# Bias of layer h of a graph layer: two matmuls on TensorE, or a table of columns added by ScalarE

## The reference

```python
h = relu(layernorm(x))
S = h[src]                                     # one row per edge
def edge_nn(x, W, b):
    h = relu(x @ W.T + b)                      # "layer h"
    return relu(h @ W.T + b)                   # "layer m"
msgs = edge_nn(S, W_rel[rel], b_rel[rel])      # rel of each edge is 0 or 1
agg = segment_sum(msgs, dst)
i, f, g, o = split(agg @ W_ih.T + b_ih + b_hh)
hn = sigmoid(o) * tanh(sigmoid(i) * tanh(g))
return x + mlp(hn)                             # 256 -> 128 -> 128 -> 256
```

## Time and profile before

| | |
|---|---|
| median of 3 runs | 2260.63 us (2260.33 to 2261.53) |
| the profiled execution | 2269.79 us, its span 2268.1 us |
| PE busy | 2080.7 us, 92% |
| DVE busy | 1755.9 us, 77% |
| ACT busy | 1627.2 us, 72% |
| POOL busy | 1187.8 us, 52% |
| mean granted TensorE clock | 0.959 of full |
| moved by DMA | 396.90 MB, mean 175 GB/s |

### The profile page before, as it was taken

How to read it: one execution, slowest core, us unless ns; L and a number is a source line. 1 busy time by engine, 2 the same in 40 slices (tenths; PEclk the granted TensorE clock), 3 DMA queues, 4 the chain that set the end, 5 groups by cost and what they waited for, 6 DMA issues and landing times.

```text
span 2268.1 us, 51837 instructions
## 1 busy us (share of the span) xinstructions
PE 2080.7 (92%) x14224; PEld 1405.7 (62%) x14225; DVE 1755.9 (77%) x4311; ACT 1627.2 (72%) x3364; POOL 1187.8 (52%) x917
## 2 busy tenths in 40 slices
PE   5858767767999999999999999999999999999996
PEld 4746555555666666666666666666666666445553
DVE  8537555555888888888888888888888887788886
ACT  2437655555888888888888888888888887666663
POOL 0036777777766665666666666666666644100000
PEclk7559999898999999999999999999999999999998
DMA  9954555557789898889888988888888988988886
GB/s 383 425 207 93 95 95 100 98 97 141 135 174 185 170 180 174 179 170 175 175 178 173 178 177 180 178 178 183 170 178 175 180 153 162 193 188 191 190 188 156
DMA packets 400606, 396.90 MB, mean 175 GB/s; under 512 B 263738, under 2 KB 343158, under 8 KB 394360
## 3 DMA queue, kind: packets, MB, share of 16 engines
q0 software_dynamic: 91200, 157.34, 40.8%
q1 hardware_dynamic: 306788, 238.12, 40.0%
q10 hardware_dynamic: 2516, 0.14, 0.1%
HBM read 185.88 MB, written 156.97 MB: 151 GB/s over the span
## 4 chain that ended last, share of the span: by engine, by line
PE 78%; issue 7%; POOL 5%; ACT 3%; DMA 3%; DVE 3%; another core or an unknown queue 1%; POOLq 0%; DVEq 0%; ACTq 0%; SPq 0%
PE bank L1469 33%; PE bank L1435 9%; PE bank L1416 9%; PE bank L1483 6%; PE bank L1508 5%; PE bank L1452 4%; PE bank L1398 3%; PE bank L1492 3%; POOL agg L664 2%; POOL xg L648 2%; DMA agg<-summed,scatter_idx 2%; PE bank L1308 2%; PE bank L1409 2%; PE bank L1427 1%; DMA a_lo<-row_lo 1%
## 5 line engine op out<-in xcount | busy, mean ns | idle before, releaser
L664 POOL DMA_INDIRECT agg<-summed,scatter_idx x400 | 665.5, 1664 | 501.4 <-ACT summed L724 261.4
L1469 PE MATMUL bank<-a_hi,ihT 128*128 128x512 f16 x2400 | 714.0, 379 | 2.4 <-DMA a_lo<-row_lo 2.2
L648 POOL DMA_INDIRECT xg<-in_x,src_ring x400 | 426.1, 1065 | 271.0 <-DMA src_ring<-src_slot 138.1
L1469 PE MATMUL bank<-a_lo,ihT 128*128 128x512 f16 x1200 | 454.8, 379 | 0.0
L1469 PEld LDWEIGHTS bank<-a_hi,ihT 128*128 128x128 f16 x2400 | 234.4, 98 | 213.0 <-issue 2.3
L1435 PE MATMUL bank<-relT,h_hi 128*128 x1600 | 321.5, 275 | 0.0
L1416 PE MATMUL bank<-s_hi,relT 128*128 128x256 f16 x1600 | 292.9, 278 | 0.0
L672 POOL DMA_DIRECT2D y<-in_x x100 | 133.4, 1334 | 298.0 <-DVE y L1202 287.6
L1077 DVE SCALAR_TENSOR_TENSOR h_lo<-bank,h_hi 128x512 f16<-128x512 f32 x200 | 137.5, 688 | 120.4 <-ACT h_hi L751 114.6
L757 ACT ACTIVATE xn<-xg,shift,rstd 128x256 f32<-128x256 f32 x400 | 216.4, 591 | 10.3 <-DVE shift L1111 10.3
L1070 DVE SCALAR_TENSOR_TENSOR s_lo<-bank,s_hi 128x512 f16<-128x512 f32 x200 | 136.4, 682 | 111.2 <-ACT s_hi L730 73.4
(11 more groups left out here) (197 smaller groups left out, 4642.4 us busy)
## 6 DMA issues: line engine op xcount, KB each, us to landing
agg_in<-agg SPq DMA_DIRECT2D x100, 512.0 KB
y<-in_x POOLq DMA_DIRECT2D x100, 512.0 KB
out<-y SPq DMA_DIRECT2D x100, 512.0 KB
agg<-zeros SPq DMA_DIRECT2D x24, 2112.0 KB, 15.8
dst_ring<-dst_rows SPq DMA_DIRECT2D x200, 128.0 KB
xg<-in_x,src_ring POOLq DMA_INDIRECT x400
agg<-summed,scatter_idx POOLq DMA_INDIRECT x400
src_ring<-src_slot SPq DMA_DIRECT2D x200, 1.0 KB
```

Of the source, the lines that this page charges most:

```text
L648: nc.gpsimd.indirect_dma_start(out=xg[:, k.slot(8), t, :], out_offset=None, in_=x[:, :], in_offset=bass.IndirectOffsetOnAxis(ap=src_ring[: ...
L664: nc.gpsimd.indirect_dma_start(out=agg[:, :], out_offset=bass.IndirectOffsetOnAxis(ap=scatter_idx[:, k.slot(8), t:t + 1], axis=0), in_=sum ...
L1469: last = nc.tensor.matmul(N_C[c % 2][:, 0:UNIT], lhs, rhs, start=i == 0, stop=i == len(todo) - 1)
```

## The change

In joint steps PE no longer adds layer h's bias. A table `pair_bias` of 400 columns is made once, two columns per pair, each with 128 features of the bias of that pair's relation. ACT applies Relu with such a column as bias, one instruction for each of the two column halves, into a new f32 tile `h_f` in SBUF (one buffer). DVE casts `h_f` to `h_hi` and subtracts to get `h_lo`. PE's wait for the bank is then on `h_f_ready`, ACT's write of `h_f` waits until DVE has made `h_lo` of the pair before, and DVE's cast waits for `m_done` of two pairs before. On DVE the cast comes ahead of `hidden`, and `low_h` moves behind it. Edge-only steps, and layer m's bias, stay as they are. In the diff the first `high_h` is ACT's, `low_h`, the second `high_h` and the table are DVE's, and `layer_h` is PE's.

```diff
-WEIGHT_LOADS = 14
+WEIGHT_LOADS = 15
...
+            act.dma_start(brel_col[:, :, :], b_rel.rearrange("r (c p) -> p r c", p=P)).then_inc(weights_in, 16)
...
             def high_h(k):
                     act.wait_ge(h_done, k.n + 1)
-                    nc.scalar.activation(h_hi[:, k.slot(2), :], B_H[k.bank][:, :], ACT.Relu).then_inc(h_hi_ready, 1)
+                    if k.both:
+                        if k.is_(NB):
+                            act.wait_ge(pair_bias_ready, 1)
+                        act.wait_ge(h_ready, k.n)
+                        for m in range(KH):
+                            half = slice(m * PAIR, (m + 1) * PAIR)
+                            last = nc.scalar.activation(h_f[:, half], B_H[k.bank][:, half], ACT.Relu,
+                                                        bias=pair_bias[:, bass.ds(k.n * KH + m, 1)])
+                        last.then_inc(h_f_ready, 1)
+                    else:
+                        nc.scalar.activation(h_hi[:, k.slot(2), :], B_H[k.bank][:, :], ACT.Relu).then_inc(h_hi_ready, 1)
...
+            chained(alternate)
+            nc.vector.tensor_scalar(other_rel[:, :], pair_rel[:, :], 0.0, None, ALU.is_equal).then_inc(pair_rel_ready, 1)
+            dve.wait_ge(pair_rel_ready, 1)
+            dve.wait_ge(weights_in, 16 * WEIGHT_LOADS)
+            for m in range(KH):
+                last = nc.vector.tensor_scalar(other_bias[:, :, m], other_rel[:, :], brel_col[:, 0, m:m + 1], None, ALU.mult)
+            chained(last)
+            for m in range(KH):
+                last = nc.vector.scalar_tensor_tensor(out=bias_of[:, :, m], in0=pair_rel[:, :], scalar=brel_col[:, 1, m:m + 1],
+                                                      in1=other_bias[:, :, m], op0=ALU.mult, op1=ALU.add)
+            last.then_inc(pair_bias_ready, 1)
...
             def low_h(k):
+                    if k.both:
+                        dve.wait_ge(h_hi_ready, k.n + 1)
+                        nc.vector.tensor_tensor(h_lo[:, k.slot(2), :], h_f[:, :], h_hi[:, k.slot(2), :],
+                                                ALU.subtract).then_inc(h_ready, 1)
...
+            def high_h(k):
+                if k.within(PAIRS):
+                    dve.wait_ge(h_f_ready, k.n - NB + 1)
+                    wait_from(dve, m_done, k.n - 1)
+                    nc.vector.tensor_copy(h_hi[:, k.slot(2), :], h_f[:, :]).then_inc(h_hi_ready, 1)
...
+                if (at - 1).both:
+                    high_h(at - 1)
+                hidden(k, half)
                 low_h(at - 1)
-                hidden(k, half)
...
             def layer_h(k, r):
-                wait_from(pe, h_ready, k.n if k.both else k.n - 1)
+                if k.is_(NB):
+                    pe.wait_ge(h_ready, k.n)
+                elif k.both:
+                    pe.wait_ge(h_f_ready, k.n - NB)
+                else:
+                    wait_from(pe, h_ready, k.n - 1)
...
-                    nc.tensor.matmul(ps, brel_parts[:, bass.ds(r * D + m * P, P)], ones16[:, :], start=True, stop=False)
+                    if not k.both:
+                        nc.tensor.matmul(ps, brel_parts[:, bass.ds(r * D + m * P, P)], ones16[:, :], start=True, stop=False)
...
-                        last = nc.tensor.matmul(ps, lhs, rhs, start=False, stop=i == len(todo) - 1)
+                        last = nc.tensor.matmul(ps, lhs, rhs, start=k.both and i == 0, stop=i == len(todo) - 1)
```

More of the change, by code:

```diff
@@ L218, in build @@
         spare_row = sb("spare_row", [P, 2])
-        pair_start = sb("pair_start", [1, PAIRS])
+        pair_start = sb("pair_start", [P, PAIRS])
         iota_tile = sb("iota_tile", [P, TILES])
@@ L228, in build @@
         dst_slot = sb("dst_slot", [P, TILES])
-        pair_rel = sb("pair_rel", [1, PAIRS], I32)
+        pair_rel = sb("pair_rel", [P, PAIRS], I32)
+        pair_bias = sb("pair_bias", [P, PAIRS * KH])
         unit_row = sb("unit_row", [1, UNITS], I32)
@@ L243, in build @@
         gate_b = sb("gate_b", [P, 8])
+        brel_col = sb("brel_col", [P, NUM_REL, KH])
         b1_col = sb("b1_col", [P, 1])
@@ L295, in build @@
         quarter_row = tmp("quarter_row", [1, QUARTERS])
-        flips = tmp("flips", [1, 2, PAIRS])
+        flips = tmp("flips", [P, 2, PAIRS])
+        other_rel = tmp("other_rel", [P, PAIRS])
+        other_bias = tmp("other_bias", [P, PAIRS, KH])
         slot = tmp("slot", [ROWS, COLS])
@@ L360, in build @@
         s_lo = sb("s_lo", [P, 2, KH * PAIR], F16)
+        h_f = sb("h_f", [P, KH * PAIR])
         h_hi = sb("h_hi", [P, 2, KH * PAIR], F16)
@@ L401, in build @@
         pair_rel_ready = sem("pair_rel_ready")
+        pair_bias_ready = sem("pair_bias_ready")
         unit_row_ready = sem("unit_row_ready")
@@ L430, in build @@
         h_done = sem("h_done")
+        h_f_ready = sem("h_f_ready")
         h_hi_ready = sem("h_hi_ready")
@@ L1075, in low_h @@
                 if k.within(PAIRS):
[L1076 to L1079, removed]
+                    if k.both:
[3 more added lines that the diff above has]
+                    else:
+                        dve.wait_ge(h_hi_ready, k.n + 1)
+                        nc.vector.scalar_tensor_tensor(out=h_lo[:, k.slot(2), :], in0=B_H[k.bank][:, :], scalar=0.0,
+                                                       in1=h_hi[:, k.slot(2), :], op0=ALU.max,
+                                                       op1=ALU.subtract).then_inc(h_ready, 1)
+            def high_h(k):
[3 more added lines that the diff above has]
+                    nc.vector.tensor_copy(h_hi[:, k.slot(2), :], h_f[:, :]).then_inc(h_hi_ready, 1)
             def spread_of(k):
```

6 lines of the change are left out of this document (3 added, 3 removed).

## The result

The changed kernel takes 2312.11 us in the median of 4 runs (2311.72 to 2315.49). The kernel before took 2261.08 us beside it (4 runs). The ratio is 1.0225, with an interval of 1.0207 to 1.0243: it is slower by 51 us, where 30 us faster was predicted. The profiled execution had 2311.72 us, its span 2310.1.

The account below looks back on a forecast made before the run. The prediction took PE to bound the joint part: -30.8 us for the removed bias matmuls and +0.3 us for the first square-root steps give -30.5, so 2230.1 us from a median of 2260.63, range 2226 to 2242.

Parts of the forecast that it names:

- What bounds the kernel: Joint part, 600 to 1900 us: PE is busy 1299.86 of 1300 us, so whatever it does less of is saved.
- What is removed: Layer h's bias matmuls on PE in joint steps: two per pair, 0.219 us, for 141 pairs, a gain of 30.8 us.
- What ACT gets: Two Relus of 256 columns into `h_f` per step, 480 ns each: +0.30 us taken, bounds +0.14 and +0.50.
- What DVE gets: A cast of `h_hi`, 445 ns, per step, with `h_lo` keeping its price: 0.25 us more work per step.
- The margins: Square-root steps: 0.18 us left before PE's third chunk needs ACT's `g_i`, 0.34 between DVE's `mean_var` and ACT's `std`.
- its rule (x - 0.52) x 35: An added x on the path to `g_i` stalls PE by x - 0.52 us in one step of four, 35 times.
- The rest: First part: about five more DVE instructions for the table, some 2 us, covered by DVE's 17.70 us wait for `mixed`.
- Its own time and the median: Profiled execution of before, 2269.79 us, would become 2239.3; taking off 9.2 us above the median gives 2230.1.
- Where it could still become late: Search for where PE waits soonest, ACT's `g_i` behind the square root; only 0.3 us counted back, for 556 to 600 us.
- the slower one: A POOL scatter holds DVE's added cast ahead of `std` for 1.61 us in 35 groups, 38 us: 2268 us, chance 0.04.
- The small stall in each square-root step: `g_i` late by 0.1 to 0.6 us in 35 steps, 4 to 20 us back: about 2240 us, chance 0.15.
- transfers bound the steps: DMA is the hidden clock, two steps need 19.32 us whatever PE does: no change, 2260 us, chance 0.03.

Follow-up runs that it names:

- run 12: Changed kernel with 48 idle DVE instructions ahead of the loop and layer h's bias matmuls kept on PE (bias added twice): 2263.89 us, ratio 1.0005 to the kernel before.
- run 1: Changed kernel with 48 idle DVE instructions ahead of the loop: 2235.52 us, ratio 0.9878 to the kernel before.
- run 9: Changed kernel, unpadded, without DVE's covered wait for `m_done` ahead of the cast of `h_hi`: 2235.24 us, ratio 0.9874 to the kernel before.
- Run 7: Changed kernel with 48 idle DVE instructions ahead of the loop and `h_f` in eight Relus of 64 columns per pair: 2250.2 us, ratio 0.9902 to before.
- run 5: Changed kernel with 12 idle DVE instructions ahead of the loop: 2294.6 us, one run.
- run 6: Changed kernel with 24 idle DVE instructions ahead of the loop: 2293.41 us, one run.
- run 8: Kernel before with 24 idle instructions in its DVE loop (294 in all) and 88 ahead of it: 2273.08 us, ratio 1.0001 to the kernel before.
- run 2: Changed kernel with 128 idle DVE instructions ahead of the loop: 2312.74 us, one run.
- run 3: Kernel before with its DVE loop padded to the changed kernel's length (294) and place (40 idle instructions ahead): 2329.99 us, ratio 1.0299 to the kernel before.
- run 10: Kernel before with only 68 idle DVE instructions ahead of its loop of 270: 2329.26 us, ratio 1.0294 to the kernel before.
- run 11: Kernel before with only 58 idle DVE instructions ahead of its loop of 270: 2262.35 us, one run.
- run 4: Kernel before without layer h's bias matmuls in joint steps, the bias left out, ACT and DVE unchanged: 2243.22 us, ratio 0.9903 to the kernel before.

## Why the prediction was wrong

*What bounds the kernel*: right. PE bounds the joint part, and what it does less of is saved.

*What is removed*: right. Two steps take 18.88 us; run 12 against run 1 gives 28.7 us by the medians and 0.219 us per step, where 30.8 and 0.219 stood in the sum.

*What ACT gets*: right. `h_f` takes 462 ns (480 predicted). Two take 0.71 us up to the next instruction's start (as 1013.37 to 1014.09 on ACT in run 1), +0.24 against 0.48 before; +0.30 was taken, inside its bounds. The groups of run 1, 600 to 1840 us (answer to the earlier trace rows):

```profile
L766 ACT ACTIVATE h_f<-bank,pair_bias 128x256 f32<-128x256 f32 x262 | 107.6, 462 | 0.0
L1110 DVE TENSOR_TENSOR h_lo<-h_f,h_hi 128x512 f16<-128x512 f32 x132 | 90.2, 684 | 0.0
L1123 DVE CAST h_hi<-h_f 128x512 f16<-128x512 f32 x131 | 55.6, 424 | 61.3 <-ACT h_f L766 61.3
```

*What DVE gets*, as work: right. The cast takes 424 ns (445 predicted), `h_lo` 684 (681).

*The margins*: the mechanisms were right. ACT's timeline at the square root, then DVE's, of after (answers to the earlier trace rows):

```profile
1171.30 0.69 ACT L796 ACTIVATE g_o<-bank,gate_b 128x512 f32<-128x512 f32 x1 [0.22 <-PE bank L1519]
1174.13 0.69 ACT L815 ACTIVATE x<-bank,b_col 128x512 f32<-128x512 f32 x1 [0.45 <-PE bank L1533]
1176.13 0.30 ACT L752 ACTIVATE std<-mean_var,eps 128x8 f32<-128x8 f32 x1
```

```profile
1175.67 0.23 DVE L1128 BATCH_NORM_AGGREGATE mean_var<-stats 128x2 f32<-128x6 f32 x2
```

The idle time ahead of `g_o` shrank from 0.68 to 0.22 and swallowed `h_f`; `x` still starts with PE. `mean_var` ends at 1175.90, 0.23 ahead of `std` (0.34 predicted). PE waits once for `g_i` in run 9. Run 7 tests the arithmetic: its `h_f` add x = 1.57 - 0.48 - 0.30 = 0.79 us to what the prediction had counted, and by its rule (x - 0.52) x 35 = 9.5 us. It was 5 to 7.

*The rest*: DVE's wait for `mixed` shrank from 17.70 to 15.97, which covers the table, as said. *Its own time and the median*: the profiled execution of before was 9.2 us above the median. The waits of ACT, 100 to 560 us of before, show one of 12.7 us that the changed kernel's profile lacks:

```profile
ACT h_hi L751 <- remote: 12.7, 1, 12.7
```

So step 60 begins at 547.09 and not 555.04 in after, which is no gain of the change. The traces of runs 5 to 8 have such a wait too (8.9 to 12.4 us, step 60 from 555.76 on), and before took 2271.68 beside them, not 2263.59. The other traces lack it. What it waits for the profile doesn't show.

*The step that failed* is "Where it could still become late": "Engines wait in order, so I looked for the place where PE waits soonest". I asked only whether an engine becomes late by the durations of its work. In "What DVE gets" the new waits, the register work and the new instructions' places counted as nothing. 24 more instructions in the loop's body and 40 more ahead of it cost no time as such, but they move the loop over a border of what DVE holds. 13 jumps x 6.1 us = 79.4 us; less 139 steps x 0.219 = 30.4 us that is +49 us, against +51 measured. From the traces: steps 60 to 199 take 1936.5 - 547.09 = 1389.4 us in after and 1895.02 - 555.04 = 1340.0 before, +49.4.

*The rivals*: the slower one had its sign right and its mechanism wrong. No cast was held for anything like a scatter's length: `h_hi`'s took 424 ns in the mean and 483 at most in run 1, 626 at most in after. The small stall in each square-root step did not come. Nor did transfers bound the steps.

Shown by runs: that place and length of DVE's loop decide (1, 2, 3, 8, 10, 11), that the removed matmuls give the predicted gain (1, 9, 12), that the added work is free (12). Shown by the traces: that a jump back waits for a packet on q14. Argued only: which piece each packet is, and that four pieces are held, one of them being loaded ahead. Open: where exactly between 379 and 385 the border lies, and why run 4 had its late transfer.

## What to carry to other kernels

An edit in an unrolled loop changes how many instructions the body has and where it begins, waits and register work included, and both can decide over more time than the edit itself. Count them in the built program. After the run look at the packets of the instruction queue, and at idle time put down to "issue" at the first instruction behind the jump, before any theory on the work. Where a kernel with a right idea comes out slower, take out a wait that another covers or shift the loop by a part of a piece (here 48 did it, 12, 24 and 128 did not), and only then judge it.

## What the runs showed of the hardware

- DVE waits 4.8 to 6.2 us in the mean at a jump back of the loops that lie past the border (7.8 in run 10, with its second wait), and 67 packets of 8 KB more are loaded for 13 of them. It was free up to 379 instructions from the start of the loop's first piece to the loop's end, and not from 385 on; three pieces of 128 are 384.
- The Trainium skill (Runtime: NRT & Kernel Launch, Instruction fetch mechanics) says that such an engine holds 32 KiB of its program and that a taken branch whose target isn't there waits for a fetch. The traces agree with the wait: 13 of 13 jumps. The section gives blocks of 16 KiB, 256 instructions, two of them held. Here the measurement differs for DVE: a shift of 128 leaves the waits as they were, where one of 48 removes them (runs 2 and 1), and the packets of q14 are of 8 KB.
- Two waits on semaphores go into one idle instruction of DVE (96 waits move the loop by 48 places in run 1); a wait dropped took 8 instructions out of 8 steps (run 9).
- Eight Relus of 64 columns with a bias column take 366 ns each, 0.20 us from start to start (1.57 / 8), where one of 256 takes 462 ns, 0.36 from start to start (0.71 / 2).
